# Last batch's transposed adjacency rounded by GpSimd's transfers, identity products in the tail, the head's first rows by quarters

## The reference, cut to what matters

```
v, q, k = relu(x @ W* + b*)
att     = softmax(q k^T where adj is 1, else -9e15)
x       = layernorm(x + relu(att v @ Wo + bo))

h       = x @ W_w^T + W_b;   e = h @ a1;   f = h @ a2
u       = adj * exp(e_i + f_j + a_b)
x       = layernorm(x + (u / rowsum(u)) @ h)
```

## Time and profile before

| | us |
|---|---|
| median of 3 runs (402.74 to 403.55) | 403.34 |
| the profiled execution | 404.14 |
| its span, first to last instruction | 402.1 |

### The profile page before, as it was taken

The page is one execution under the profiler, slowest core; times in us unless marked ns, Lnnn a source line. Parts: engine busy times, 40 slices in busy tenths (PEclk is TensorE's granted clock), DMA queues, the critical chain, the costliest instruction groups (busy, mean ns, idle before and its releaser), DMA issues.

```text
span 402.1 us, 8861 instructions
## 1 busy us (share of the span) xinstructions
PE 385.1 (96%) x2758; PEld 358.3 (89%) x2758; DVE 345.4 (86%) x1053; ACT 331.4 (82%) x660; POOL 280.7 (70%) x258
## 2 busy tenths in 40 slices
PE   8999999999999999999999999999999999999790
PEld 7789988999999989999899999999899999999790
DVE  4897898899789997989879998899969998987856
ACT  5887679998789887997879888898879979997672
POOL 1653951697358994699928996589948898782753
PEclk9999999999999999999999999999999999999786
DMA  8808616818557259736588077663486369777011
GB/s 268 317 12 313 198 31 216 330 42 288 185 185 287 107 190 289 275 138 218 178 275 324 4 286 217 227 268 121 153 280 260 130 214 360 234 246 257 2 55 52
DMA packets 37869, 80.72 MB, mean 201 GB/s; under 512 B 2752, under 2 KB 19264, under 8 KB 37824
## 3 DMA queue, kind: packets, MB, share of 16 engines
q1 hardware_dynamic: 37680, 80.03, 57.0%
q10 hardware_dynamic: 144, 0.14, 0.2%
HBM read 75.96 MB, written 4.19 MB: 199 GB/s over the span
## 4 chain that ended last, share of the span: by engine, by line
PE 82%; DVE 6%; ACT 5%; issue 3%; DMA 3%; POOL 0%; SPq 0%; POOLq 0%; DVEq 0%; ACTq 0%
PE m_ps L1744 12%; PE pt_ps L1696 12%; PE s_ps L1628 7%; PE s_ps L1630 7%; PE s_ps L1629 7%; PE av_ps L1708 7%; PE av_ps L1710 6%; PE av_ps L1709 6%; PE m_ps L1635 6%; PE m_ps L1636 2%; PE m_ps L1628 2%; PE m_ps L1629 2%; PE m_ps L1630 2%; DMA adjt_in<-in_adj_t_dram 2%; PE m_ps L1725 2%
## 5 line engine op out<-in xcount | busy, mean ns | idle before, releaser
L657 ACT ACTIVATE prob_th<-pt_ps 128x512 fp32r<-128x512 f32 x128 | 74.6, 596 | 18.7 <-PE pt_ps L1696 18.4
L1011 DVE CUSTOM_DVE_ANT_0 prob<-s_ps,penalty 128x1024 f32<-128x1024 f32 x64 | 77.8, 1216 | 13.1 <-PE s_ps L1630 6.5
L393 POOL TENSOR_SCALAR penalty<-raw 128x1024 bf16<-128x1024 f32 x64 | 66.4, 1046 | 32.5 <-DMA raw<-in_adj_dram 12.8
L1019 DVE TENSOR_TENSOR prob_tl<-pt_ps,prob_th 128x512 fp32r<-128x512 f32 x128 | 85.6, 681 | 3.6 <-ACT prob_th L657 3.4
L649 ACT ACTIVATE prob<-prob,neg_max 128x1024 f32<-128x1024 f32 x64 | 73.8, 1153 | 3.7 <-DVE neg_max L1011 3.6
L1696 PE MATMUL pt_ps<-rhs,prob 128*128 128x128 f32 x512 | 74.2, 273 | 0.0
L1708 PE MATMUL av_ps<-prob_th,vh 128*128 128x256 f32 x256 | 73.3, 286 | 0.0
L1710 PE MATMUL av_ps<-prob_th,vl 128*128 128x256 f32 x256 | 72.3, 283 | 0.0
L1709 PE MATMUL av_ps<-prob_tl,vh 128*128 128x256 f32 x256 | 72.3, 282 | 0.0
L595 ACT ACTIVATE adj_t<-adjt_in 128x1024 fp32r<-128x1024 f32 x56 | 59.4, 1061 | 12.8 <-PE m_ps L1744 11.8
L1744 PE MATMUL m_ps<-g,adj_t 128*128 128x258 f32 x448 | 63.8, 288 | 0.7 <-ACT adj_t L595 0.3
(11 more groups left out here) (157 smaller groups left out, 923.0 us busy)
## 6 DMA issues: line engine op xcount, KB each, us to landing
raw<-in_adj_dram SPq DMA_DIRECT2D x64, 512.0 KB, 5.7
adjt_in<-in_adj_t_dram SPq DMA_DIRECT2D x56, 512.0 KB, 3.9
raw<-in_x_t_dram SPq DMA_DIRECT2D x16, 256.0 KB, 4.2
x_in<-in_x_dram SPq DMA_DIRECT2D x8, 512.0 KB, 6.5
raw<-in_adj_t_dram SPq DMA_DIRECT2D x8, 512.0 KB, 6.6
out_dram<-out_sb SPq DMA_DIRECT2D x14, 256.0 KB, 4.3
out_dram<-out_sb SPq DMA_DIRECT2D x4, 128.0 KB, 1.8
wb<-in_pack_b_dram SPq DMA_DIRECT2D x1, 320.0 KB, 4.3
```

The costliest lines, as they stand in the source:

```text
L657: sc.activation(prob_th[n % 2][:, tiles(k), (i % 2) * P:(i % 2 + 1) * P], pt_ps[k][:, :].rearrange("p (c n) -> p c n", n=P), ACT.Copy).the ...
L1011: v.tensor_tensor_reduce(out=prob[i % 2][:, :], in0=s_ps[:, :, :].rearrange("p a n -> p (a n)"), in1=penalty[:, n % RING, :], scale=-1.0, ...
L1019: v.tensor_tensor(prob_tl[n % 2][at], pt_ps[k][:, :].rearrange("p (c n) -> p c n", n=P), prob_th[n % 2][at].bitcast(F32), ALU.subtract).th ...
```

## The change: what it does

- The last batch's transposed tiles are loaded by GpSimd's queue, from the float32 tensor in HBM straight into the float32r tile `adjt_last`, so that the transfer converts. `round_last` and its eight places on ScalarE are gone, as are the eight loads in SP's list. The waits for the space are the same. `aggregate_first` waits for the arrival.
- `hold_clock` runs four identity products on TensorE into `pt_ps[0]`; it stands once after `attend(LAST, 3)` and twice after `transpose_x1_pair(3)`.
- In the head the first half of x transposed comes as two quarters of 128 KB with their own high and low parts and products, `wa` as two transfers (Wq first), and Wq and Wk are split separately. `wb` is loaded after x, x of batch 1 before the second adjacency tile.
- The lists of all engines are in another order in the head and in the tail. The list of the middle passes is as it was.

```diff
+    HOLD = 4
@@ SP
-            def load_adj_last(i):
-                if i >= RING:
-                    sp.wait_ge(penalty_done, T * LAST + i + 1)
...
-                sp.dma_start(raw[:, i, :], adj_t_tiles[LAST, i].rearrange("p t d -> p (t d)")).then_inc(adjt_last_arrived[i], 16)
+            def load_x_t_quarter(r):
+                sp.dma_start(quarter(xt_in, r), quarter(x_t[0], r)).then_inc((xt_quarter, xt_arrived[0])[r], 16)
             def head():
-                load_x_t(0, 0)
+                load_x_t_quarter(0)
+                load_x_t_quarter(1)
+                load_x_t(0, 1)
                 load_wb()
-                load_x_t(0, 1)
                 load_adj(0, 0)
                 load_x(0)
+                load_x_t(1, 0)
+                load_x_t(1, 1)
                 load_adj(0, 1)
...
@@ GpSimd
+            def load_adj_last(i):
+                if i >= RING:
+                    pool.wait_ge(penalty_done, T * LAST + i + 1)
+                elif i == 3:
+                    pool.wait_ge(vl_done, 2 * B)
+                else:
+                    pool.wait_ge(*lower((xtl_done, ql_done, kl_done)[i], LAST, 1))
+                gp.dma_start(adjt_last[:, i, :, :], adj_t_tiles[LAST, i]).then_inc(adjt_last_arrived[i], 16)
...
                 convert(LAST, 4)
+                load_adj_last(0)
+                load_adj_last(1)
+                v_lo(LAST, 1)
+                load_adj_last(2)
+                residual1(LAST - 2, 0)
+                residual1(LAST - 2, 1)
                 convert(LAST, 5)
                 convert(LAST, 6)
...
+                convert(LAST, 7)
                 add_wb(LAST - 1)
                 g_lo(LAST - 1, 0)
+                load_adj_last(3)
+                load_adj_last(4)
                 g_lo(LAST - 1, 1)
                 rstd1_pow(LAST - 2)
                 norm1(LAST - 2, 0)
-                convert(LAST, 7)
+                load_adj_last(5)
                 norm1(LAST - 2, 1)
                 rstd0_pair(0)
+                load_adj_last(6)
                 rstd0_pair(1)
+                load_adj_last(7)
                 residual1(LAST - 1, 0)
                 residual1(LAST - 1, 1)
-                add_wb(LAST, 0)
...
                 norm1(LAST - 1, 1)
+                add_wb(LAST, 0)
                 add_wb(LAST, 1)
@@ ScalarE
-            def round_last(i):
-                act.wait_ge(adjt_last_arrived[i], 16)
-                sc.activation(flat(adjt_last[:, i, :, :]), raw[:, i, :], ACT.Copy).then_inc(adjt_last_done, 1)
+            def first_x_hi(r):
+                act.wait_ge((xt_quarter, xt_arrived[0])[r], 16)
+                sc.activation(quarter(xth, r), quarter(xt_in, r), ACT.Copy).then_inc((xth_quarter, xth_done)[r], 1)
...
-            sc.dma_start(wa[:, :], pack_a).then_inc(wa_arrived, 16)
+            sc.dma_start(blk(wa, 0), blk(pack_a, 0)).then_inc(wq_arrived, 16)
+            sc.dma_start(wa[:, D:2 * D + 8], pack_a[:, D:2 * D + 8]).then_inc(wa_arrived, 16)
@@ VectorE, the head's order
+                split_in(0)
+                first_x_lo_quarter(0)
+                split_in(1)
+                first_x_lo_quarter(1)
+                split_vo()
+                first_x_lo(1)
                 place_rhs1()
+                v_bias(0, 0)
+                v_sum(0, 0)
                 first_q_lo(0)
                 first_k_lo(0)
+                v_bias(0, 1)
                 first_k_lo(1)
+                v_sum(0, 1)
+                centre_w()
                 mask_max(0, 0)
...
@@ TensorE
-                pe.wait_ge(adjt_last_done, i + 1)
+                pe.wait_ge(adjt_last_arrived[i], 16)
...
+            def hold_clock():
+                pe.wait_ge(ptl_done, 2 * T * B - 1)
+                for _ in range(HOLD):
+                    pe.matmul(pt_ps[0][:, 0:P], ident, ident, start=True, stop=True)
...
+                transpose_x1_pair(2)
                 attend(LAST, 3)
-                transpose_x1_pair(2)
+                hold_clock()
                 project_out_pair(3)
                 project_h_pair(2)
                 aggregate_first(0)
                 transpose_x1_pair(3)
+                hold_clock()
+                hold_clock()
                 aggregate_first(1)
+                project_h_pair(3)
                 aggregate_first(2)
-                project_h_pair(3)
...
```

More of the change, by code:

```diff
@@ L170, in half, with quarter @@
             return ap[:, k * HALF:(k + 1) * HALF]
+        def quarter(ap, r):
+            return ap[:, r * PAIR:(r + 1) * PAIR]
         def blk(ap, i):
@@ new lines, in tail @@
+                agg_out(LAST - 2, 7)
+                den_out(LAST - 2)
+                inv_den_out(LAST - 2)
+                prob_lo(LAST, 2, 0)
+                scale_out(LAST - 2)
+                prob_lo(LAST, 2, 1)
+                mask_max(LAST, 4)
+                x1_lo(LAST - 1, 0)
+                stats1(LAST - 2, 0)
+                mean_var1(LAST - 2, 0)
+                h_out(LAST - 1, 0)
+                h_out(LAST - 1, 1)
+                inverse_sum_pair(0)
+                av_lo(LAST, 0)
@@ L1500, in tail @@
                 h_out(LAST - 1, 7)
-                o_bias(LAST, 0)
+                prob_lo(LAST, 4, 0)
+                residual0(LAST, 0)
                 stats1(LAST - 2, 1)
-                o_sum(LAST, 0)
-                mean_var1(LAST - 2, 0)
+                mask_max(LAST, 6)
+                g_lo_den(LAST - 1)
+                mean_var1(LAST - 2, 1)
+                prob_lo(LAST, 4, 1)
+                av_lo(LAST, 1)
                 inverse_sum_pair(1)
-                mean_var1(LAST - 2, 1)
@@ L1537, in tail @@
-                var_eps0_pair(1)
+                x1_lo_pair(0)
+                stats0_pair(0)
+                mean_var0_pair(0)
+                o_bias(LAST, 1)
+                prob_lo(LAST, 5, 0)
+                prob_lo(LAST, 5, 1)
+                o_sum(LAST, 1)
+                var_eps0_pair(0)
+                mask_max(LAST, 7)
+                residual0(LAST, 1)
+                agg_out(LAST - 1, 0)
+                stats0_pair(1)
+                agg_out(LAST - 1, 1)
+                mean_var0_pair(1)
@@ L1538, in tail @@
+                x1_lo_pair(1)
+                var_eps0_pair(1)
+                agg_out(LAST - 1, 2)
+                prob_lo(LAST, 6, 0)
+                av_lo(LAST, 2)
+                inverse_sum_pair(2)
+                agg_out(LAST - 1, 3)
+                agg_out(LAST - 1, 4)
+                prob_lo(LAST, 6, 1)
+                o_out_pair(2)
+                residual0_pair(2)
+                prob_lo(LAST, 7, 0)
+                inverse_sum_pair(3)
                 agg_out(LAST - 1, 5)
-                prob_lo(LAST, 7, 0)
+                stats0_pair(2)
@@ L1551, in tail @@
+                g_lo_pair(0)
                 stats1(LAST - 1, 0)
-                g_lo_pair(0)
                 g_lo_pair(1)
-                mean_var0_pair(2)
                 mean_var1(LAST - 1, 0)
+                av_lo(LAST, 3)
                 g_lo_den_pair(0)
+                stats1(LAST - 1, 1)
+                g_lo_den_pair(1)
                 var_eps0_pair(2)
-                av_lo(LAST, 3)
-                stats1(LAST - 1, 1)
-                x1_lo_pair(2)
                 mean_var1(LAST - 1, 1)
@@ L1644, in shared, with first_project_q @@
                 return bank[what, b, part]
+            def first_project_q(r):
+                pe.wait_ge(set_ok, 1)
+                pe.wait_ge((xtl_quarter, xtl_done[0])[r], 1)
+                q = quarter(shared("q", 0, 0), 0) if r == 0 else quarter(bank["q", 0, 0], 1)
+                last = product(q, (wqh, wql), (quarter(xth, r), quarter(xtl, r)))
+                if r == 1:
+                    last.then_inc(q_full, 1)
             def project_q(b, k):
```

453 lines of the change are left out of this document (194 added, 259 removed), and 6 rows, old and new, of the table HEAD_SLOTS.

## The result

The changed kernel takes **404.97 us** (median of 7 runs), the kernel before 403.34 in the same comparison: ratio **1.0052, 95% interval [1.0029, 1.0074]**. It is slower by half a per cent; the prediction said 398.9, and 403.2 at the most. The forecast was wrong in its sign.

What follows compares the result with a forecast made beforehand. Middle passes were taken as bound by TensorE's work, the tail by whoever feeds it; 0.5 + 1.0 + 0.9 + 2.06 = 4.5 us off the 402.1 span gave 397.6, so a median of 398.9 us, range 396.6 to 403.2.

Steps and rivals of the forecast that it cites:

- Part 1: Tail before the last attend: GpSimd's converting loads replace ScalarE's roundings; 1.0 us gained, bounds 0 to 1.5.
- Both covers hold, so I book 0: GpSimd's tail list: with its issues, v_lo(LAST, 1) still comes 1.5 us and convert 5 0.6 us early; no cost.
- 1.5 us of waiting: TensorE from 318.44 to 372.66 us: work priced at 52.6 of 54.2 us, only about 1.5 us waiting.
- Rival E: Tail transfers collide: GpSimd's loads 3 to 7 share the engines with the last staged loads; 400.9 to 402.0 us, chance 0.15.
- The issue on GpSimd: GpSimd's tail list: each load issue takes 1.1 us, 8.8 in all, between 0.33 and 2.39 us each.
- Rival C: Tail: GpSimd becomes the bound at 2.39 us an issue; 6.3 us lost against 4.5 gained, 405.1 us, chance 0.13.
- Worth of the freed ScalarE: Tail: eight roundings of 1.05 us go, freeing 7.6 us of ScalarE; 1.0 us of it counted as gain.
- Part 2: Last stop, after the last attend: shorter wait gains 0.9 us, clock held by identity products gains 2.06 us.
- The clock was to hold: Wait before project_out_pair(3): four identity products leave TensorE only 0.6 us idle, so the clock is held.
- The next stretch: From project_out_pair(3) to the end of project_h_pair(3): 4.95 us instead of 7.01, a gain of 2.06.
- The end: After project_h_pair(3), with VectorE's last chain of 11.5 us: 0 gained (−0.5 to +0.5).
- Part 3: Head: first product 1.1 us sooner, near 5.3, first mask_max at 13.2; 0.5 us gained (−0.3 to 1.1).

Runs made afterwards that it cites:

- e7: Changed kernel with GpSimd's convert(LAST, 7) put back behind norm1(LAST - 2, 0); 403.31 us, ratio 1.0004 to the kernel before.
- e9: Changed kernel with convert(LAST, 7) back behind norm1(LAST - 2, 0) and only the first four of twelve identity products; 401.96 us, ratio 0.9965 to before.
- e10: e9 with the head of the kernel before; 401.92 us, ratio 0.9962 to the kernel before.
- e6: Changed kernel with GpSimd's loads 0 to 2 behind convert(LAST, 7) and 5 to 7 after the last staged tile's rounding; 403.08 us, ratio 1.0007 to before.
- e11: e10 with GpSimd's loads 5 to 7 behind the rounding of the last staged tile; 401.74 us, ratio 0.9960 to the kernel before.
- e5: Kernel before with GpSimd's eight converting loads, no ScalarE roundings, other lists as before, no identity products; 403.99 us, ratio 1.0020 to before.
- e15: e9 with the eight loads on SP's queue and the roundings on ScalarE again; 407.93 us, ratio 1.0109 to the kernel before.
- e3: Changed kernel without its twelve identity products; 405.17 us, ratio 1.0053 to the kernel before.
- e14: Kernel before with four identity products ahead of project_out_pair(3), nothing else; 402.62 us, ratio 0.9987 to the kernel before.
- e8: Changed kernel with its lists, but SP loads into the raw buffer and ScalarE rounds; 408.22 us, ratio 1.0137 to the kernel before.
- e2: Kernel before with the changed tail alone; 404.82 us, ratio 1.0041 to the kernel before.
- e12: Changed kernel with 8 warm-up products instead of 11; 405.28 us, ratio 1.0050 to the kernel before.

## Why the prediction was wrong

It forecast a span of 397.6 where 403.2 was measured: 5.6 us. By its own terms:

- **Part 1, the failed step: "Both covers hold, so I book 0".** The walk over the two lists ended at mask_max(LAST, 5). One step further stand convert(LAST, 6) and convert(LAST, 7), and behind them add_wb(LAST − 1), which was in front of convert(LAST, 7) before. The walk priced GpSimd's instructions and not the transfers for which they wait (1.43 and 1.51 us). Booked was 1.0 gained, measured 4.2 lost: a difference of 5.2 us, nearly all of the error. By the runs it falls into four. 2.3 to 2.4 come with convert(LAST, 7) (e7, e9, e10). About 1.4 are lost in the new lists even without it, and which move costs them was not tried. 0.4 are the two transposes, whose price the prediction took out of the last stop (it counts the idle time there from 375.6, where they begin) and booked nowhere else. And the gain of 1.0 was taken from 1.5 us of waiting, a remainder of a sum; the profile's own list shows one wait of 0.3 in that stretch. Rival E had another part, the staged load caught among GpSimd's loads (7.82 us where it was 6.18), but priced it all at 2 to 3 and put 0.15 on it. e6 shows that this wait was real; e7 and e11 that it goes with the convert, whether the loads give way or not; what makes that load slow stays open.
- **The issue on GpSimd** was taken at 1.1 us and bounded by 2.39; the eight take 0.53 to 0.76, 0.59 in the median. Rival C named the right engine as the one that delays the work, and for the wrong reason: it ended at nearly the measured time (405.1) with issues at 2.39 us, and they cost half of what even the forecast had taken. That was luck.
- **Worth of the freed ScalarE.** In the old lists GpSimd's loads alone gain nothing (e5, 1.0020, expected 0.9975). In the mended lists, taking them away costs 6 us (e15 against e9; 2 to 3.5 expected), but a part of that is the early first rounding and the clock. So what this term is worth stays open; the two runs show only that it depends on the order around it.
- **Part 2, right in its sum, not in its terms.** Attend to project_out_pair(3) was to gain 0.9 and gained 1.15, with the two transposes out of it; without their 0.4 it is 0.75. The clock was to hold, and does, in every execution. The next stretch was to take 4.95 and takes 5.79: the excess is mainly aggregate_first(0) with a wait of 0.36 us for VectorE's x behind it (1.06 us where 0.48 was booked). The eight identity products were put at 1.76, with 0.5 of waiting to be taken off. They take 1.70 by their starts, and taking them out saves 1.00 (e3, e9), because a wait of 0.5 us for x1tl comes in their place. The term also compared unlike stretches: the old 7.01 holds three aggregates, the new list two. e14 shows that in the lists of before, four products alone bring 0.13%, less than can be told, and leave 1.06 us idle, after which the mean clock is still low in 7 of 12 executions.
- **The end** was booked at 0 and gained 0.77 us (17.04 to 16.27, 16.20 in e9), although it has one aggregate more, 0.5 us at full clock; e14, with the old lists, has no such gain (17.16). It comes with the new order; which of its moves does it was not separated. Together with the stretch before, 1.99 us were gained where 2.06 were booked, two errors that cancel.
- **Part 3** was booked at 0.5 gained; the tail starts 0.04 later. Its first mask_max, forecast at 13.2 "So the chain of the first tiles does not move", is at 13.44, and the work moved out of TensorE's way is worth nothing that shows: in all these kernels the tail starts between 318.1 and 319.0, with either head.

So the range failed because its slower side hung on one mechanism's price (the issue). The convert's wait for its transfer was in no rival, and the staged load's had 0.15.

## What to carry to other kernels

When an instruction that waits for a transfer moves ahead of work with a reader, price the transfer's landing and not the instruction: follow the engine's list until nothing behind it is needed, not until the first cover holds. A reading of "so much of this stretch is waiting" that is left over from a sum wants the profile's list of waits beside it. Stretches are compared only when they hold the same work. Filler products for the clock are free only inside a wait that exists: four that left 0.2 us of a wait of 1.1 kept the clock in all 12 executions, the same four in the old lists, which left 1.06 us, did not, and eight in a place with 0.5 us of waiting cost 1.0 us. And an edit that puts work back on another engine has to be checked for the same fault that it is to test: e8 and e15 each held a rounding that waited for its transfer.

## What the runs showed of the hardware

An issue of a converting 512 KB load takes GpSimd 0.53 to 0.76 us, less than an elementwise instruction of 128x512 (1.04). Such a load lands in 7.8 us in the median where five of them share the engines with the staged loads, issued from 355 to 372 us:

```profile
adjt_last<-in_adj_t_dram POOLq DMA_DIRECT2D x5, 512.0 KB, 7.8
adjt_in<-in_adj_t_dram SPq DMA_DIRECT2D x3, 512.0 KB, 5.2
```

The one queue of before had 7.6 for its four plain loads there; over all eight it is 7.4 against 6.6 on the pages. In e7, with the convert back, the five take 5.4 in the same stretch. So the time to land depends on the lists as much as on the kind of load, and a price of converting in flight can't be read from these runs.

And a fall of the granted clock differs from execution to execution of one kernel. Counting executions by their mean clock, with the idle time in front of project_out_pair(3) of the profiled one: after 1.1 us it came in 5 of 12 executions of three kernels and in 7 of 12 of a fourth, after 2.08 us in 107 of the 122 of the kernel before in all four batches, and after 0.19 to 0.26 us (after, e2, e6, e7, e9 to e12) in one of 91. It isn't told by the length of the wait alone.
